# Scheduling edit in a two-layer attention and FFN kernel: fill work, transfers and context turns move to other slots

## The chip, the cores and the metric

The kernel runs on one core of one Trainium2 chip. The time is the device time in microseconds (us) of one execution; lower is better. Engines are named as the profile names them: PE (TensorE), DVE (VectorE), ACT (ScalarE), POOL (GpSimd), SP (SyncE, which issues most DMAs). PEld is PE's weight load.

## The reference, cut to what matters

Two recurrent layers over `x` of shape (2, 512, 512). Layer 0, the one that the change touches, is causal attention with 32 heads of 16 columns and rotary position, times the SiLU of a gated FFN:

```python
xn = _layernorm(x)
q, k, v = split(xn @ qkv_w + qkv_b)           # heads of 16, q and k rotated
probs = softmax(q @ k.T / 4 + causal mask)     # 32 heads, 512 x 512
s = (probs @ v) @ out_w + out_b
g = silu((silu(xn @ W_gate.T) * (xn @ W_up.T)) @ W_down.T)
x = x + s * g
```

Layer 1 (a recurrent convolution stack as "attention" and an octonion ternary FFN) has the same outer form. It takes the time from about 485 us on, and no edit touches it.

## The kernel before, in words

`program` writes one instruction stream by hand for each engine. Layer 0 is done for batch entry b = 0 and then b = 1 (called block 0 and block 1 below).

**Weights as units.** The float32 weights come in 49 units of 128x512 per block. SP loads unit n into `raw[n % 4]` (`load`, L639) once unit n-4 is ready; a high part is made by ACT (`split_hi`, L1263) or by POOL (`split`, L737), and POOL subtracts it for the low part (L745), which makes the unit ready. `HI_BY_ACT` (L178) says up to which unit ACT makes the high part. `w_hi` and `w_lo` have five buffers, so unit n also waits until unit n-5 is used. A product of float32 quality is three matmuls (`passes`, L929: high x high, high x low, low x high); one unit over one of four row chunks is a *triple*, and a unit of Q, K or FFN is four triples.

**Order within a block.** PE does Q unit 0 and K unit 1 of the first eight heads, then the V units 2 to 5, then the first units of `Q_UNIT`, `K_UNIT` and `FFN_UNIT` (L55, L56) "in front" (`fill(b, -1)`, L1027; units 6, 7 and 8, 12 triples, all three FFN). Then come slots s = 0 to 64 (`SLOTS`, L51). Slots 0 to 47 each hold one third of a head pair's scores: PE writes `score_ps` (`scores`, L953) as soon as DVE has taken the row maxima of the slot before from it (`part_ready`, L1037), DVE takes the maxima (`row_maxima`, L1456), and after every third slot joins them (L1467) for PE to turn (`max_turn`, L938). Five slots later PE makes the transposed scores (`scores_T`, L962), ACT takes the exponentials (L1316), POOL masks them (`keep_causal`, L756). After its scores each slot gets *fill*: the triples that `triple_slot` (L80) gives to it, mostly two, in some slots one. When unit u's last triple is in slot s, DVE and ACT do its epilogue in slot s+1: `ffn_tanh` on ACT and `ffn_out` on DVE for the FFN, `rope_first` (three DVE instructions) for Q and K and `rope_second` one slot later. `units_after(s)` lists them. An FFN unit with an even place in `FFN_UNIT` needs ACT's tanh before DVE's `ffn_out`, one with an odd place does not. PE's fill for a unit waits (L988) until the unit two jobs earlier has left its PSUM bank, that is for `ffn_out` or `rope_first` of that one (`proj_free`).

**Stacks.** The rotated Q and K rows go to memory (`write_rows`, L647, in slot `written_in`) and come back as one stack of q and k for each group of four heads (`read_rows`, L657: four DMAs of 200 KB, in slot `read_in`, L113). Group g is needed by PE's scores in slot 6g, which wait for it (L1036). SP does everything in program order, so a load that waits for its unit holds the reads behind it. Group 2 comes from Q and K units 9 and 10; its read is in slot 9, and its scores are in slot 12.

**Context.** `pv_in` gives the product of probabilities and V to slots 12+6g to 15+6g. In slot 16+6g ACT copies it to `ctx_sums` (L1323), in slot 17+6g PE turns that (L1067 to L1070) and DVE divides by the sums (L1590, L1592).

**Down phase.** From slot 54 PE does W_down, one unit f per slot (`down_in`, L117), on `hsh`/`hsl`, which ACT and DVE split from `hidden_T` two slots ahead (L1339, L1607); ACT's split for f needs `down_used` of f-2. PE starts when DVE's first split is there (L1055). The last context groups are turned in slots 53 and 59. ACT makes the high parts of the units that lie behind by `DOWN_HI` (L248).

In these slots PE's order is written out as follows:

```python
fill(b, s)                                       # L1047
max_turn                                         # L1048
down_in(s): wait hs_ready, unit_ready; passes    # L1053
ctx_in(s): wait ctx_copied; turn                 # L1067
pv_in(s)                                         # L1071
```

## Time and profile before

| quantity | value |
|---|---|
| median of 3 runs | 715.39 us |
| lowest, highest | 712.02, 716.94 us |
| profiled execution: its own time | 716.94 us |
| profiled execution: span of its instructions | 715.2 us (1.7 us lie around it) |
| mean granted TensorE clock | 0.97 of full speed |
| PE busy | 637.2 us, 89% of the span |
| DVE, POOL, ACT busy | 433.3, 387.4, 290.9 us |

The profile is of one execution. A timeline row gives the start, the duration, engine, line, operation and the tiles written and read; in brackets stands the idle time of that engine before the row and what ended it. A row of SPq is a DMA issue, and its duration is the issue alone. Matmul ends are modelled, so the distance from one start to the next is the safer figure for them. Stage by stage: the front of block 0 ends at 47.87 us, its slots with scores and fill run to about 197 us, its down phase to 237 us; block 1 has the same at 275, 431 and 470 us.

### The profile page before, as it was taken

What the parts mean: (1) busy time and instruction counts of PE and PEld (TensorE: products, weight loads), DVE (VectorE), ACT (ScalarE), POOL (GpSimd) and SP (SyncE); (2) the same over time, 40 slices, a digit from 0 to 9 for tenths busy, and PEclk for the clock granted to TensorE, in tenths of its full rate; (3) what the DMA queues carried; (4) which work ended last, traced back from release to release, by engine and by line L of the source; (5) the groups of instructions that cost most, each with busy time, mean ns of one, the idle gap of its engine ahead of it and who ended that gap; (6) DMA issues with size and microseconds to landing.
All of it is one profiled execution on the core that took longest, in us unless ns stands there. A gap on an engine that the chain in (4) does not pass through costs nothing. (4 is left out here: it accounts for less than half of the span.)

```text
span 715.2 us, 9831 instructions
## 1 busy us (share of the span) xinstructions
PE 637.2 (89%) x3293; PEld 432.8 (61%) x3293; DVE 433.3 (61%) x1016; ACT 290.9 (41%) x475; POOL 387.4 (54%) x553
## 2 busy tenths in 40 slices
PE   2988899999999998779999999997989799797993
PEld 1855555666567785446566656776765576555671
DVE  4849868666345765966866634567364424657347
ACT  2523545455634430445455553432124334141531
POOL 4665556544333755644645433479426786634465
PEclk9999999999999999989999999999989989999997
DMA  8486755644322335975464337145000000000003
GB/s 287 137 296 189 213 171 162 174 129 103 104 60 66 96 118 164 306 221 167 130 192 134 93 119 301 60 156 184 1 1 0 0 1 1 0 1 0 1 0 117
DMA packets 59906, 83.26 MB, mean 116 GB/s; under 512 B 17848, under 2 KB 26296, under 8 KB 59856
## 3 DMA queue, kind: packets, MB, share of 16 engines
q1 hardware_dynamic: 56192, 71.35, 33.5%
q10 hardware_dynamic: 3664, 11.28, 4.1%
q8 instruction: 26, 0.43, 0.2%
q14 instruction: 24, 0.20, 0.1%
HBM read 64.80 MB, written 26.99 MB: 128 GB/s over the span
## 5 line engine op out<-in xcount | busy, mean ns | idle before, releaser
L745 POOL TENSOR_TENSOR w_lo<-raw,w_hi 128x512 fp32r<-128x512 f32 x98 | 129.7, 1329 | 86.6 <-ACT w_hi L1269 82.2
L1463 DVE CUSTOM_DVE_ANT_0 score_ps<-score_ps,causal 128x512 f32<-128x512 f32 (+3 forms) x256 | 119.8, 515 | 57.0 <-PE score_ps L958 56.5
L1316 ACT ACTIVATE probs_T<-scoreT_ps 128x1024 f32<-128x1024 f32 (+1 forms) x96 | 84.8, 883 | 80.6 <-PE scoreT_ps L967 79.8
L930 PE MATMUL proj_ps<-xn_hi,w_hi 128*128 128x512 f32 x224 | 101.0, 451 | 4.7 <-POOL w_lo L745 2.5
L931 PE MATMUL proj_ps<-xn_hi,w_lo 128*128 128x512 f32 x224 | 89.3, 399 | 0.0
L932 PE MATMUL proj_ps<-xn_lo,w_hi 128*128 128x512 f32 x224 | 89.3, 399 | 0.0
L743 POOL TENSOR_SCALAR w_hi<-raw 128x512 fp32r<-128x512 f32 x50 | 31.0, 620 | 90.4 <-PE proj_ps L932 78.5
L930 PEld LDWEIGHTS proj_ps<-xn_hi,w_hi 128*128 128x128 f32 x224 | 42.4, 189 | 30.2 <-issue 13.1
L958 PE MATMUL score_ps<-k_st,q_st 50*128 50x512 f32 (+3 forms) x256 | 44.7, 386 | 16.9 <-DVE row_max L1463 13.4
L765 POOL TENSOR_SCALAR_AFFINE_SELECT probs_T<-probs_T 128x256 f32<-128x256 f32 x128 | 50.0, 413 | 17.2 <-ACT probs_T L1316 17.1
L958 PEld LDWEIGHTS score_ps<-k_st,q_st 50*128 50x128 f32 x256 | 21.6, 184 | 58.8 <-issue 28.1
L932 PEld LDWEIGHTS proj_ps<-xn_lo,w_hi 128*128 128x128 f32 x224 | 42.9, 192 | 10.1
L1081 PE MATMUL ctx_ps<-probs_T,V 128*32 128x128 f32 (+3 forms) x512 | 47.7, 445 | 0.0
L885 POOL TENSOR_TENSOR hsL<-hidden_T,hsH 128x256 fp32r<-128x256 f32 x44 | 34.8, 803 | 22.2 <-ACT hsH L1402 22.1
L1238 ACT ACTIVATE q_st<-one_turn_ps 2x512 fp32r<-2x512 f32 x64 | 37.4, 584 | 22.0 <-PE one_turn_ps L944 21.7
L931 PEld LDWEIGHTS proj_ps<-xn_hi,w_lo 128*128 128x128 f32 x224 | 42.9, 191 | 5.0
L1516 DVE SCALAR_TENSOR_TENSOR gate_silu<-gate_tanh,proj_ps 128x512 f32<-128x512 f32 x22 | 15.1, 685 | 44.0 <-ACT gate_tanh L1278 38.2
L967 PE MATMUL scoreT_ps<-q_st,k_st 50*128 50x512 f32 (+3 forms) x256 | 37.7, 331 | 1.8 <-ACT probs_T L1316 1.8
L1607 DVE TENSOR_TENSOR hsl<-hidden_T,hsh 128x512 fp32r<-128x512 f32 x22 | 17.0, 771 | 34.6 <-ACT hsh L1339 34.6
L1269 ACT ACTIVATE w_hi<-raw 128x512 fp32r<-128x512 f32 x48 | 29.9, 624 | 17.5 <-PE one_turn_ps L932 6.5
L1247 ACT ACTIVATE rows_hi<-turned_rows 128x512 fp32r<-128x512 f32 x16 | 10.1, 632 | 65.2 <-DVE turned_rows L1544 60.2
L754 POOL TENSOR_TENSOR rows_lo<-turned_rows,rows_hi 128x512 fp32r<-128x512 f32 x16 | 20.8, 1299 | 27.7 <-ACT rows_hi L1247 27.7
(310 smaller groups left out, 1444.8 us busy)
## 6 DMA issues: line engine op xcount, KB each, us to landing
raw<-w SPq DMA_DIRECT2D x98, 256.0 KB, 2.8
rows<-rows_hi SPq DMA_DIRECT2D x32, 256.0 KB, 3.4
arranged<-tern SPq DMA_DIRECT2D x96, 85.0 KB
q_st<-rows SPq DMA_DIRECT2D x32, 200.0 KB
k_st<-rows SPq DMA_DIRECT2D x32, 200.0 KB
rows<-rows_lo SPq DMA_DIRECT2D x16, 256.0 KB, 4.1
gate_w<-arranged ACTq DMA_DIRECT2D x4, 704.0 KB, 7.0
up_w<-arranged ACTq DMA_DIRECT2D x4, 704.0 KB, 7.8
```

The lines of the kernel that those rows point to most:

```text
L745: nc.gpsimd.tensor_tensor(w_lo[n % SPLIT][:, :], raw[n % RAW][:, :], F32(w_hi[n % SPLIT][:, :]), ALU.subtract).then_inc(unit_ready, 1)
L765: m = nc.gpsimd.affine_select(out=halves[:, :, c:c + P], in_=halves[:, :, c:c + P], pattern=[[0, 2], [1, P]], compare_op=ALU.is_ge, fill=0 ...
L885: nc.gpsimd.tensor_tensor(hsL[d % HS][:, :], hidden1_T[:, f, 256 * pr:256 * pr + 256], F32(hsH[d % HS][:, :]), sub).then_inc(hs1_ready, 1)
L930: nc.tensor.matmul(acc, lh, rh, start=first, stop=False)
L931: nc.tensor.matmul(acc, ll, rh, start=False, stop=False)
L932: return nc.tensor.matmul(acc, lh, rl, start=False, stop=last)
L958: m = nc.tensor.matmul(score_ps[:, hh, c:c + (qt + 1) * P], q[:, qt * P:(qt + 1) * P], k[:, 0:(qt + 1) * P], start=part == 0, stop=True, s ...
L967: m = nc.tensor.matmul(scoreT_ps[:, hh, c:c + S - kt * P], k[:, kt * P:(kt + 1) * P], q[:, kt * P:], start=part == 0, stop=True, skip_grou ...
L1081: m = nc.tensor.matmul(ctx_ps[32 * h:32 * h + 32, kt * P:S], V[:, kt, (4 * g + h) * 32:(4 * g + h + 1) * 32], probs_T[(gp + h // 2) % 4][: ...
L1238: m = nc.scalar.activation(q_st[g % 3][64 * hh:64 * hh + 2, j % 2, :], turn_bank(n)[32 * hh:32 * hh + 2, :], ACT.Copy)
L1316: nc.scalar.activation(probs_T[gp % 4][:, c:c + 2 * w].rearrange("p (h c) -> p h c", h=2), scoreT_ps[:, :, 0:w], ACT.Exp, scale=0.25).then ...
L1463: m = nc.vector.tensor_tensor_reduce(out=block, in0=block, in1=causal[:, S - w:], scale=1.0, scalar=-3e38, op0=ALU.add, op1=ALU.max, accum ...
```

## The change

Nine edits, which the diff shows in full:

1. Units 8 and 9 become the second Q and K unit (they were 9 and 10), unit 10 becomes FFN. Eight triples stand in front instead of 12, and the 104 others are spread over the 53 slots. The four that leave the front go to slots 8, 17, 35 and 44, which then hold two triples instead of one. The Q and K units of groups 2 and 3 end in slots 1 and 3 as before; the units behind them up to unit 29 end one slot later, with two exceptions: unit 11 ends in slot 7 (unit 10, FFN now, in slot 5) and unit 12 in slot 9 instead of 7.
2. Group g is read 7 slots after its K unit instead of 6: group 2 in slot 10 instead of 9; the other groups stay in their slots.
3. POOL makes the high parts of units 6, 7 and 8 too.
4. In each slot SP issues the raw loads before the row writes and the stack reads. With edit 1 the load in slot 10 is that of unit 21, which waits for unit 17, and unit 17's split waits for PE's last triple of unit 12 in slot 9. Slot 0 holds seven loads instead of eight.
5. PE turns the context right behind the scores of a slot, ahead of fill and down.
6. PE waits for the last `proj_free` at the first down unit (slot 54) instead of ahead of `norm_turn` (slot 60).
7. ACT copies the context after the tanh, rope, maximum, `hsh` and `DOWN_HI` work of the slot instead of ahead of it.
8. DVE does the `ffn_out` of the front units in slot 0, behind the row maxima of slot 0, instead of ahead of slot 0.
9. ACT no longer makes a high part between the two `rope_hi` of the front.

```diff
--- before.py
+++ after.py
@@ -52,9 +52,8 @@
 
 U_DOWN, U_OUT = 34, 45
 UNITS = U_OUT + KC
-Q_UNIT, K_UNIT, V_UNIT = (0, 9, 12, 18), (1, 10, 13, 19), 2
-FFN_UNIT = [6, 7, 8, 11, 14, 15, 16, 17] + list(range(20, 34))
-IN_FRONT = 3 * KC
+Q_UNIT, K_UNIT, V_UNIT = (0, 8, 12, 18), (1, 9, 13, 19), 2
+FFN_UNIT = [6, 7, 10, 11, 14, 15, 16, 17] + list(range(20, 34))
 FILL = 6
 TRIPLES = (U_DOWN - FILL) * KC
 JOBS = U_DOWN - KC
@@ -79,7 +78,7 @@
 
 def triple_slot(k):
 
-    return max(-1, (k - IN_FRONT) * SCORE_SLOTS // (TRIPLES - IN_FRONT))
+    return max(-1, (k - 2 * KC) * SCORE_SLOTS // (TRIPLES - 2 * KC))
 
 
 def triples_in(s):
@@ -111,7 +110,7 @@
 
 
 def read_in(s):
-    return next((g for g in range(1, GROUPS) if (1 if g == 1 else max(6 * g - 6, unit_slot(K_UNIT[g // 2]) + 6)) == s), None)
+    return next((g for g in range(1, GROUPS) if (1 if g == 1 else max(6 * g - 6, unit_slot(K_UNIT[g // 2]) + 7)) == s), None)
 
 
 def down_in(s):
@@ -175,7 +174,7 @@
 TURN_BANK = turn_banks()
 
 
-HI_BY_ACT = FILL + 3
+HI_BY_ACT = FILL
 RAW_HEAD = 10
 RAW, SPLIT = 4, 5
 COPIES = (50, 49)
@@ -694,12 +693,12 @@
                         write_rows(b, K_UNIT[0])
                         read_rows(b, 0)
                 for s in range(SCORE_SLOTS + 1):
+                    for u in raw_in_slot(s):
+                        load(b, u)
                     for u in written_in(s):
                         write_rows(b, u)
                     if read_in(s) is not None:
                         read_rows(b, read_in(s))
-                    for u in raw_in_slot(s):
-                        load(b, u)
                     if b == 0 and s == 3:
                         write_edges(1)
                     for x in range(copies_in(b, s)):
@@ -1044,6 +1043,10 @@
                         if s > LAG:
                             pe.wait_ge(probs_ready, TASKS * b + s - LAG)
                         scores_T(b, j, x)
+                    if ctx_in(s) is not None:
+                        g = ctx_in(s)
+                        pe.wait_ge(ctx_copied, GROUPS * b + g + 1)
+                        turn(b, ("ctx", g), [ctx_sums[:, t * P:(t + 1) * P] for t in range(NT)])
                     fill(b, s)
                     if max_in(s) is not None:
                         max_turn(b, max_in(s))
@@ -1056,6 +1059,7 @@
                         pe.wait_ge(unit_ready, UNITS * b + U_DOWN + f + 1)
                         if f == 0:
                             pe.wait_ge(probs_ready, TASKS * (b + 1))
+                            pe.wait_ge(proj_free, JOBS * (b + 1))
                         wh, wl = unit(b, U_DOWN + f)
                         for t in range(NT):
                             c = slice(t * P, (t + 1) * P)
@@ -1064,10 +1068,6 @@
                     if s == LAST_DOWN:
                         for kc in range(2, KC):
                             turn(b, ("ctxf", kc), [ctx_rows[:, t, kc * P:(kc + 1) * P] for t in range(NT)])
-                    if ctx_in(s) is not None:
-                        g = ctx_in(s)
-                        pe.wait_ge(ctx_copied, GROUPS * b + g + 1)
-                        turn(b, ("ctx", g), [ctx_sums[:, t * P:(t + 1) * P] for t in range(NT)])
                     if pv_in(s) and pv_in(s)[1] < NT:
                         g, kt = pv_in(s)
                         gp = PAIRS * b + 2 * g
@@ -1084,7 +1084,6 @@
                         if kt == NT - 1:
                             m.then_inc(pv_done, 1)
                     if s == NORM_TURN:
-                        pe.wait_ge(proj_free, JOBS * (b + 1))
                         norm_turn(b + 1)
 
                 for kc in range(KC):
@@ -1284,13 +1283,10 @@
                 split_hi(u)
             magnitudes()
             for b in range(B):
-                for u in range(5 if b else RAW, FILL):
+                for u in range(5 if b else RAW, HI_BY_ACT):
                     split_hi(UNITS * b + u)
                 rope_hi(b, Q_UNIT[0])
-                split_hi(UNITS * b + FILL)
                 rope_hi(b, K_UNIT[0])
-                for u in range(FILL + 1, HI_BY_ACT):
-                    split_hi(UNITS * b + u)
                 act.wait_ge(ones_set, 2 + b)
                 for i in range(NT):
                     act.wait_ge(v_done, NT * b + i + 1)
@@ -1315,12 +1311,6 @@
                         w, c = WIDTH[x], t_col(0, x)
                         nc.scalar.activation(probs_T[gp % 4][:, c:c + 2 * w].rearrange("p (h c) -> p h c", h=2), scoreT_ps[:, :, 0:w], ACT.Exp,
                                              scale=0.25).then_inc(probs_ready, 1)
-                    if pv_in(s) and pv_in(s)[1] == NT:
-                        g = pv_in(s)[0]
-                        act.wait_ge(pv_done, GROUPS * b + g + 1)
-                        if g:
-                            act.wait_ge(turned, use(b, ("ctx", g - 1)) + 1)
-                        nc.scalar.activation(ctx_sums[:, :], ctx_ps[:, :], ACT.Copy).then_inc(ctx_copied, 1)
                     for u in units_after(s):
                         if u in FFN_OF:
                             ffn_tanh(b, u)
@@ -1340,6 +1330,12 @@
                     for u in range(U_DOWN, UNITS):
                         if s == DOWN_HI[u - U_DOWN]:
                             split_hi(UNITS * b + u)
+                    if pv_in(s) and pv_in(s)[1] == NT:
+                        g = pv_in(s)[0]
+                        act.wait_ge(pv_done, GROUPS * b + g + 1)
+                        if g:
+                            act.wait_ge(turned, use(b, ("ctx", g - 1)) + 1)
+                        nc.scalar.activation(ctx_sums[:, :], ctx_ps[:, :], ACT.Copy).then_inc(ctx_copied, 1)
                     if s == TASKS:
 
                         act.wait_ge(rows_lo_ready, 8 * (b + 1))
@@ -1571,8 +1567,6 @@
                         dve.wait_ge(tern_a, w + 1)
                         nc.vector.scalar_tensor_tensor(out=tern_neg[w][:, :], in0=tern_w[w][:, :], scalar=theta[:, 1, w:w + 1], in1=tern_over[w][:, :],
                                                        op0=ALU.is_lt, op1=ALU.subtract).then_inc(tern_ready, 1)
-                for u in units_after(0):
-                    ffn_out(b, u)
                 for s in range(SLOTS):
                     if score_in(s):
                         row_maxima(b, s)
@@ -1596,7 +1590,7 @@
                     for u in units_after(s - 1):
                         if u in QK_OF:
                             rope_second(b, u)
-                    for u in units_after(s) if s else ():
+                    for u in units_after(s):
                         if u in FFN_OF:
                             ffn_out(b, u)
                         else:
```

## Rows read from the trace of the kernel before

**Rows 1.** Busy time by stretch: us, engines (instructions), granted clock, DMA share, GB/s.

```profile
47.87:84.87 37.00, 30.62 (x157) 19.38 (x156) 33.42 (x94) 12.92 (x18) 21.70 (x28) 1.00 0.65 200
...
275.00:318.60 43.60, 32.99 (x155) 20.80 (x155) 33.53 (x94) 14.08 (x21) 28.67 (x35) 0.92 0.72 232
...
44.20:47.60 3.40, 3.40 (x10) 2.52 (x8) 0.00 (x0) 0.00 (x0) 3.32 (x4) 0.50 1.04 411
...
310.30:317.00 6.70, 5.21 (x17) 3.34 (x16) 3.14 (x7) 1.97 (x3) 2.54 (x5) 0.51 0.93 285
```

**Rows 2.** Timeline of PE, block 0, end of the front and slots 0, 1.

```profile
43.37 0.47 PE L930 MATMUL proj_ps<-xn_hi,w_hi 128*128 128x512 f32 x1 [2.12 <-DVE gate_silu L1516]
...
47.87 0.49 PE L958 MATMUL score_ps<-k_st,q_st 50*128 50x512 f32 x2
...
50.72 0.50 PE L958 MATMUL score_ps<-k_st,q_st 50*128 50x384 f32 x4 [0.76 <-DVE row_max L1463]
```

**Rows 3.** Timeline of SP's queue: stack reads of groups 0 and 2, both blocks.

```profile
34.28 0.71 SPq L668 DMA_DIRECT2D q_st<-rows  x2
...
72.49 0.92 SPq L668 DMA_DIRECT2D q_st<-rows  x2
...
267.81 0.70 SPq L668 DMA_DIRECT2D q_st<-rows  x2
...
306.46 0.70 SPq L668 DMA_DIRECT2D q_st<-rows  x2
```

**Rows 4.** Timeline of PE, block 1: slot 0, its fill, slot 12.

```profile
274.99 0.50 PE L958 MATMUL score_ps<-k_st,q_st 50*128 50x512 f32 x2 [0.37 <-DMA k_st<-rows]
...
277.63 0.50 PE L930 MATMUL proj_ps<-xn_hi,w_hi 128*128 128x512 f32 x1 [2.14 <-POOL w_lo L745]
...
313.03 0.79 PE L958 MATMUL score_ps<-k_st,q_st 50*128 50x512 f32 x2 [1.49 <-DMA k_st<-rows]
```

**Rows 5.** Timeline of DVE, block 0: first row maxima of slot 0.

```profile
49.27 0.69 DVE L1463 CUSTOM_DVE_ANT_0 score_ps<-score_ps,causal 128x512 f32<-128x512 f32 x1
```

**Rows 6.** Timeline of ACT, block 0: exponentials of slot 6.

```profile
66.86 1.00 ACT L1316 ACTIVATE probs_T<-scoreT_ps 128x1024 f32<-128x1024 f32 x1
```

**Rows 7.** Timeline of DVE, block 0: epilogue of slot 6.

```profile
67.47 0.68 DVE L1520 TENSOR_TENSOR hidden_T<-gate_silu,proj_ps 128x512 f32<-128x512 f32 x1
```

**Rows 8.** Timeline of POOL, block 0: high part of unit 17.

```profile
70.09 0.62 POOL L743 TENSOR_SCALAR w_hi<-raw 128x512 fp32r<-128x512 f32 x1 [0.70 <-PE proj_ps L932]
```

**Rows 9.** Timeline of PE, block 0: scores of slots 10, 12, 23, 25.

```profile
76.13 0.50 PE L958 MATMUL score_ps<-k_st,q_st 50*128 50x384 f32 x4 [1.97 <-DVE row_max L1463]
...
81.15 0.50 PE L958 MATMUL score_ps<-k_st,q_st 50*128 50x512 f32 x2
...
112.98 0.39 PE L958 MATMUL score_ps<-k_st,q_st 50*128 50x256 f32 x2 [0.48 <-DVE row_max L1463]
...
120.52 0.50 PE L958 MATMUL score_ps<-k_st,q_st 50*128 50x384 f32 x4 [1.20 <-DVE row_max L1463]
```

**Rows 10.** Timeline of ACT, block 0: slot 52, then slot 58.

```profile
196.16 0.59 ACT L1323 ACTIVATE ctx_sums<-ctx_ps 128x512 f32<-128x512 f32 x1
...
215.75 0.63 ACT L1339 ACTIVATE hsh<-hidden_T 128x512 fp32r<-128x512 f32 x1 [1.67 <-PE score_ps L932]
...
216.29 0.62 ACT L1269 ACTIVATE w_hi<-raw 128x512 fp32r<-128x512 f32 x1
```

**Rows 11.** Timeline of PE, block 0: slots 53, 54, then slot 59.

```profile
196.81 0.66 PE L926 MATMUL one_turn_ps<-ident,ctx_sums 128*128 128x128 f32 x4 [0.28 <-ACT ctx_sums L1323]
...
198.12 0.50 PE L930 MATMUL score_ps<-w_hi,hsh 128*128 128x512 f32 x1 [0.66 <-DVE hsl L1607]
...
215.49 0.39 PE L930 MATMUL score_ps<-w_hi,hsh 128*128 128x512 f32 x1
...
218.22 0.60 PE L926 MATMUL one_turn_ps<-ident,ctx_sums 128*128 128x128 f32 x4
```

**Rows 12.** Timeline of DVE, block 0: slot 53.

```profile
198.61 0.68 DVE L1520 TENSOR_TENSOR hidden_T<-gate_silu,proj_ps 128x512 f32<-128x512 f32 x1
```

## The prediction, made before the changed kernel was seen

> **What bounds the kernel now.** I read the busy time by stretch first. In the slots of block 0 from 47.87 to 84.87 us PE is busy for 30.6 of 37.0 us and DVE for 33.4; in the same slots of block 1 (275.00 to 318.60) PE is busy for 33.0 of 43.6 us, at a granted clock of 0.92 [rows 1]. So the first dozen slots are not bound by PE: its idle time there ends on DVE's row maxima, on the stack read of group 2 (1.49 us at 313.03) or, in the front, on DVE and POOL [rows 2, 4, 9]. Every other stretch of layer 0 is PE's, and there each us that PE newly waits lengthens the kernel. The timelines then say which step holds PE at each place that the change touches. I work with the profiled execution (716.94 us, 1.55 above the median of 715.39) and carry the difference over to the median.
>
> **Fewer triples in front.** In block 0 PE waits 2.12 us before the third front unit, and its scores begin at 47.87 [rows 2]. After the change they can follow unit 7, which ends before the wait, at 43.37 - 2.12 = 41.25, if the stack is there. The stack of group 0 in block 1 is first issued at 267.81, and the scores that wait for it start at 274.99: 7.2 us [rows 3, 4]. From 34.28 that gives 41.5. But slot 0's fill is now unit 8, whose bank rule wants the `ffn_out` of unit 6, and DVE does that behind slot 0's row maxima. Scores 0.5; maxima 1.45 (from 49.27 to the release of slot 1 at 50.72 [rows 2, 5]); `ffn_out` 0.7 [rows 7]: PE resumes at 44.15. A triple takes 0.7: four triples of the down phase span 215.49 to 218.22 [rows 11]. Two of them put slot 1 at 45.55 instead of 50.72: **5.2 earlier**. That new wait has PE's whole queue behind it.
>
> In block 1 the stack is the limit already: 274.99 stays. The fill resumes at 274.99 + 0.5 + 1.45 + 0.7 = 277.6, where it resumed before (277.63, then for unit 9's low part [rows 4]). **Nothing is gained**, though four triples less are done.
>
> POOL's extra high parts (three of 0.62 [rows 8] per block) end before PE wants these units in block 0 and lie under the wait for the stack in block 1; ACT's freed time was idle too. Cost 0; if not covered, 3 x 0.62 = 1.9 per block.
>
> **Slots 1 to 10.** From slot 1 to slot 10 block 0 takes 76.13 - 50.72 = 25.4. Slot 10 loses its wait for row maxima of 1.97, since the rope of unit 12 moves from slot 8 to slot 10 [rows 9]. Slot 8 holds one triple more, +0.7. Slot 6 loses an epilogue that needs no tanh (DVE at 67.47) and gets one that does: ACT can make the tanh only behind its exponentials, which end at 67.86 [rows 6, 7], and with 0.6 of tanh DVE starts at about 68.4, +0.9. So 25.4 - 2.0 + 0.7 + 0.9 = 25.0: slot 10 starts at 70.6.
>
> **The read of group 2.** This is the term that speaks against the change. Before, POOL starts unit 17's high part at 70.09, as soon as PE is through with unit 12, SP loads raw unit 21 when unit 17 is ready, and the read goes out at 72.49: 2.4 us [rows 3, 8]. Now unit 12 ends two slots later, the load is in slot 10, and the read stands behind it. Unit 12 ends shortly before slot 10, so the split starts at about 70.4 and the read goes out at 72.8. The nearest flight is block 1's: issued at 306.46, scores released at 313.03, 6.6 us [rows 3, 4]; the other one is 7.2. The stack lands at 79.4, while slot 12 would be due at 70.6 + (81.15 - 76.13) = 75.6 [rows 9]. PE stands for 3.8 us, and slot 12 starts 1.75 before the 81.15 of now. Of the 5.2 gained, this is what is left.
>
> Block 1, with the same steps from 279.1 (277.6 and two triples): slot 10 at 304.1, read at 306.3, slot 12 at 312.9 against 313.03 [rows 4]. **About 0**, though its old stall was only 1.49. The row writes of unit 9 go out earlier than before there, since fewer loads stand ahead of them in slot 0; I take that as enough for the read not to wait for them.
>
> **The deferred triples.** Of the four, slot 8's is counted. The three of slots 17, 35 and 44 lie where PE doesn't wait: 3 x 0.7 = **+2.1 per block**.
>
> **The later ropes.** Units 18 and 19 move a slot on. The waits for row maxima at 112.98 (0.48) and 120.52 (1.20) [rows 9] become, with the ropes beside longer slots, about 0.6 in all: **-1.1 per block**. Bounds: 0 and -1.7. The earlier context turn frees DVE sooner in these slots, and PE doesn't wait for it, as ACT copies without tanh or rope ahead of it in them.
>
> **The down phase.** Two new waits, both on PE, and PE is the bound.
> - Slot 54 waits for the last `proj_free`. DVE's instruction for it runs from 198.61 to 199.29 (it stands behind the context work), while PE started at 198.12 [rows 11, 12]. PE starts at 199.4: **+1.3**. The turn of slot 53 gets later by one `hsh` (0.6), within this wait.
> - Slot 59: ACT's `hsh` of slot 58 can start only when PE ends slot 58 (215.75, after a wait for PE), then comes a high part to 216.91, and only then, now, the context copy of 0.59 [rows 10]: 217.5. PE wants the turn, now ahead of its down unit, at 215.49 [rows 11]. **+2.0.** Before, the copy was ahead of `hsh`, and the turn at 218.22 waited for nothing. Queued behind PE's wait are all down units left and the next block's norm turns, so nothing gives it back. Bounds for both together: 0, were the waits covered in some way, and 5.
>
> So +3.3 per block. The wait taken out of slot 60 ended nowhere: 0.
>
> **The clock.** In two stretches the granted clock is 0.50, that is the 1.2 GHz level: 44.20 to 47.60, right behind PE's wait of 2.12 (3.4 us, price 1.7), and 310.30 to 317.00 around the stall of group 2 in block 1 (6.7 less 1.49 idle, halved: 2.6) [rows 1, 2, 4]. Behind the 2.14 at 277.63 no such stretch followed. After the change the wait of block 0's front is as long, block 1's slot 12 stalls longer, and block 0's slot 12 stalls anew. I take one half-speed stretch more than now, **+1.7**; bounds 0 and five more (8.5).
> The Trainium skill ("TensorE: Matmul & The Clock Gate", section "HAM oscillation — how this bites in real kernels") says that a PE that waits for a DMA between bursts drops to the low clock, and that the next burst then starts cold each time. By it both stalls at slot 12 and the wait for the first stack of block 1 would be paid at the low clock. The rows agree for 313.03 and say nothing of a 3.8 us stall; this rule is the second rival below.
>
> **The sum.** Block 0: -1.75 + 2.1 - 1.1 + 3.3 = +2.55. Block 1: 0 + 2.1 - 1.1 + 3.3 = +4.3. Clock +1.7. Total **+8.5**: 725.4 on the profiled execution, 723.9 on the median, 1.2% slower.
>
> **The rivals.**
> 1. *The group 2 read isn't late.* If it flew in less time or were waited for by less, slot 12 would start when due: 3.8 earlier in block 0, and in block 1 at 304.1 + 5.0 = 309.1, 3.8 earlier. 8.5 - 7.6 = +0.9, 716.3: not slower. For it: the two flights differ by 0.6, so the DMA share of the moment counts, and fewer loads are queued here. Against: two flights of 6.6 and 7.2 with two slots of about 5 us to cover them. It decides from a flight below 2.8 us.
> 2. *Cold bursts.* Three more half-speed stretches than the one counted, 3 x 1.7 = +5.1: 729.0. For it: 3.8 us stalls are longer than any wait of now in these slots. Against: 277.63.
> 3. *The down phase hides its waits.* 8.5 - 6.6 = +1.9: 717.3. For it: DVE and ACT are half idle there. Against: the order of the two queues is written out, and each wait names an instruction with a row.
> 4. *Both 1 and 3*: the early start pays and nothing takes it back, 8.5 - 7.6 - 6.6 = -5.7: 709.7, faster.
>
> **How the numbers follow.** Chances: forecast 0.45, rival 1 0.17, rival 2 0.16, rival 3 0.12, rival 4 0.10. About 1% (7.2 us) is what a measurement of this kernel can tell from no change. The forecast, with some 3 us either way, is beyond 722.5 in two cases of three (0.30) and within it else (0.15); rival 2 adds 0.16 to slower, rivals 1 and 3 give 0.26 to no change and 0.03 to slower, and rival 4 is split between faster (0.06) and no change (0.04). That makes 0.49 slower, 0.45 same, 0.06 faster. The range runs from 714.5 (rival 1 with the clock's term gone) to 730.
>
> **What would show it.** PE's scores of slot 12 wait 3 to 4.5 us for the DMA `k_st` in both blocks, and SP issues the read of group 2 about 2.4 us behind POOL's start on unit 17. Slot 0's scores are at about 41.5 and 275. PE's first down matmul waits for DVE's `hidden_T`, about 2.3 us in all with the turn, and the turn of slot 59 waits 2 us for ACT's `ctx_sums`. If the down waits are absent the step on program order is wrong; if slot 12 doesn't wait, the one on the flight; if both stand and the time is beyond 730, the clock's.

## The result: 3% slower, beyond the range

| quantity | before | after |
|---|---|---|
| median | 716.16 us (4 runs, 712.02 to 720.77) | 737.43 us (4 runs, 734.84 to 739.20) |
| ratio after / before, 95% interval | | 1.029 [1.022, 1.037] |
| profiled execution, its span | 716.94, 715.2 us | 734.26, 732.5 us |
| PE busy | 637.2 us | 644.0 us |
| PE not busy (span less busy) | 78.0 us | 88.5 us |
| mean granted clock | 0.970 | 0.953 |

The forecast was 723.9 us within 714.5 to 730: the sign is right, the size is not. The medians lie 21.3 us apart and the two profiled executions 17.3; the account below is of the profiled pair, and it doesn't cover the other 4 us (the executions of one kernel lie 2 to 12 us apart). The last rows of the table split the 17.3 us by which the span grew. PE stands 10.5 us longer, and it is busy for 6.8 us longer although not one matmul was added (3293 in both). The second part is what to explain: the same matmuls took longer.

Two rows of the page of after, the totals and the slices of PE's clock:

```profile
PE 644.0 (88%) x3293; PEld 437.5 (60%) x3293; DVE 434.5 (59%) x1016; ACT 288.4 (39%) x469; POOL 392.1 (54%) x559
...
PEclk9999899999999998989999998999999989898997
```

The waits of PE in after (for what, us in total, times, longest):

```profile
PE score_ps L957 <- DMA k_st<-rows: 13.6, 3, 5.3
...
PE score_ps L957 <- DVE row_max L1459: 8.3, 10, 2.0
...
PE one_turn_ps L925 <- ACT ctx_sums L1338: 5.2, 4, 1.8
...
PE score_ps L929 <- DVE hidden_T L1516: 3.0, 2, 1.5
```

The same view of the kernel before:

```profile
PE score_ps L958 <- DVE row_max L1463: 13.4, 14, 2.0
...
PE score_ps L958 <- DMA k_st<-rows: 3.1, 3, 1.5
...
PE score_ps L930 <- DVE hsl L1607: 1.3, 2, 0.7
...
PE one_turn_ps L926 <- ACT ctx_sums L1323: 0.6, 2, 0.3
```

Waits for row maxima shrank by 5.1 us; waits for the stack grew by 10.5, and those of the down phase from 1.9 to 8.2. All three places were named in the prediction. PE's timeline of after has them one by one (start, duration, what PE did, and in brackets the idle time ahead of it); these rows answer to [rows 2, 4, 9, 11]:

```profile
40.21 0.50 PE L957 MATMUL score_ps<-k_st,q_st 50*128 50x512 f32 x2
42.84 0.77 PE L929 MATMUL proj_ps<-xn_hi,w_hi 128*128 128x512 f32 x1 [2.13 <-POOL w_lo L744]
43.40 0.63 PE L930 MATMUL proj_ps<-xn_hi,w_lo 128*128 128x512 f32 x1
43.83 0.63 PE L931 MATMUL proj_ps<-xn_lo,w_hi 128*128 128x512 f32 x1
...
45.67 0.50 PE L957 MATMUL score_ps<-k_st,q_st 50*128 50x384 f32 x2
...
79.72 0.80 PE L957 MATMUL score_ps<-k_st,q_st 50*128 50x512 f32 x2 [5.31 <-DMA k_st<-rows]
...
198.77 0.66 PE L925 MATMUL one_turn_ps<-ident,ctx_sums 128*128 128x128 f32 x4 [0.79 <-ACT ctx_sums L1338]
200.93 0.47 PE L929 MATMUL score_ps<-w_hi,hsh 128*128 128x512 f32 x1 [1.50 <-DVE hidden_T L1516]
201.23 0.39 PE L930 MATMUL score_ps<-w_hi,hsl 128*128 128x512 f32 x1
201.46 0.39 PE L931 MATMUL score_ps<-w_lo,hsh 128*128 128x512 f32 x1
...
220.20 0.65 PE L925 MATMUL one_turn_ps<-ident,ctx_sums 128*128 128x128 f32 x4 [1.78 <-ACT ctx_sums L1338]
...
280.59 0.49 PE L957 MATMUL score_ps<-k_st,q_st 50*128 50x512 f32 x2 [3.25 <-DMA k_st<-rows]
283.21 0.76 PE L929 MATMUL proj_ps<-xn_hi,w_hi 128*128 128x512 f32 x1 [2.13 <-DVE gate_silu L1512]
...
321.10 0.80 PE L957 MATMUL score_ps<-k_st,q_st 50*128 50x512 f32 x2 [5.08 <-DMA k_st<-rows]
```

Two things are to be seen. Every place holds the wait that the step on it foresaw, and the two at slot 12 are longer than reckoned. And the distance between two matmuls of one chain is not the same everywhere: 0.23 us at 201.23, 0.43 at 43.40. The second is a matmul at the low clock. The busy time by stretch shows how much of that there is; these are all half-speed stretches of layer 0 in after:

```profile
42.41:45.82 3.41, 2.98 (x8) 1.99 (x8) 0.97 (x2) 0.00 (x0) 3.24 (x5) 0.50 1.04 405
56.06:59.48 3.42, 3.42 (x11) 2.06 (x10) 3.33 (x11) 1.55 (x2) 0.81 (x1) 0.50 0.92 308
76.54:83.37 6.83, 3.65 (x12) 2.80 (x13) 3.39 (x8) 1.65 (x2) 2.39 (x4) 0.50 0.94 264
281.34:288.17 6.83, 4.96 (x13) 3.48 (x14) 3.70 (x13) 0.00 (x0) 6.50 (x8) 0.50 0.39 123
318.89:325.71 6.82, 4.61 (x16) 3.26 (x16) 3.51 (x7) 1.57 (x2) 2.38 (x4) 0.50 0.91 253
441.77:448.59 6.82, 5.83 (x16) 4.00 (x20) 1.71 (x3) 0.28 (x1) 1.17 (x1) 0.50 1.01 409
sum 34.13, PE 25.45 PEld 17.59 DVE 16.63 ACT 5.05 POOL 16.49; mean PE 4.24 PEld 2.93 DVE 2.77 ACT 0.84 POOL 2.75
```

Before had two of them, with PE busy for 3.40 + 5.21 = 8.6 us in them [rows 1]; after has six, with 25.45 us. A matmul at 1.2 GHz comes every 0.43 us and not every 0.23 to 0.24, so some 45% of this busy time is lost: 11.4 us instead of 3.9, **+7.5 us** (with a plain half, +8.4). The prediction had allowed +1.7.

The 45% hold where PE is the bound. PE's busy time in layer 0 grew by less, 5.2 us (452.1 to 457.4), so +7.5 is an upper value and +5.2 a lower one; after_again below shows where a part of the difference goes.

The account stage by stage, both profiles:

| stretch | before | after | difference |
|---|---|---|---|
| start to first scores of block 1 | 274.99 | 280.59 | +5.6 |
| block 1 to the turn of layer 1's first input | 222.6 (274.99 to 497.58) | 232.7 (280.59 to 513.28) | +10.1 |
| layer 1 | 217.6 | 219.2 | +1.6 |

The 1.6 us of layer 1 are the clock again. The sums over the half-speed stretches behind 497.58 us of before, then behind 513.28 us of after:

```profile
sum 23.89, PE 21.02 PEld 15.71 DVE 11.47 ACT 4.82 POOL 13.71; mean PE 4.21 PEld 3.14 DVE 2.29 ACT 0.96 POOL 2.74
sum 27.31, PE 24.81 PEld 19.18 DVE 12.66 ACT 7.32 POOL 14.10; mean PE 4.96 PEld 3.84 DVE 2.53 ACT 1.46 POOL 2.82
```

PE works 3.8 us more at half speed there, and 45% of that is 1.7. No kernel of this document changes layer 1, and yet it lasts 215.9 to 221.5 us in their 14 profiles. PE's work at half speed in it is 17.2 to 29.5 us, each us of it goes with 0.46 us of layer 1's length, and no profile lies more than 0.1 us off that line.

### The profile page after: what moved, and what is told of

Same layout as the page of the kernel before. It is cut to its first block and busy times, and to the rows that moved or that the text cites. A ratio compares the mean times of both kernels' runs of the same rounds, so it can differ in the third digit from the quotient of the medians.

```text
span 732.5 us, 9833 instructions
## 1 busy us (share of the span) xinstructions
PE 644.0 (88%) x3293; PEld 437.5 (60%) x3293; DVE 434.5 (59%) x1016; ACT 288.4 (39%) x469; POOL 392.1 (54%) x559
## 5 line engine op out<-in xcount | busy, mean ns | idle before, releaser
L744 POOL TENSOR_TENSOR w_lo<-raw,w_hi 128x512 fp32r<-128x512 f32 x98 | 127.8, 1307 | 95.0 <-ACT w_hi L1268 90.1
L742 POOL TENSOR_SCALAR w_hi<-raw 128x512 fp32r<-128x512 f32 x56 | 37.1, 663 | 99.3 <-PE proj_ps L931 90.5
L1237 ACT ACTIVATE q_st<-one_turn_ps 2x512 fp32r<-2x512 f32 x64 | 37.5, 585 | 26.9 <-PE one_turn_ps L943 26.4
L1246 ACT ACTIVATE rows_hi<-turned_rows 128x512 fp32r<-128x512 f32 x16 | 10.1, 631 | 75.1 <-DVE turned_rows L1540 75.1
L1459 DVE DVE_READ_ACCUMULATOR2_ANT row_max<- 128x1 f32 x256 | 35.6, 139 | 0.3
L1329 ACT ACTIVATE hsh<-hidden_T 128x512 fp32r<-128x512 f32 x22 | 13.9, 630 | 49.9 <-PE score_ps L931 49.9
L1268 ACT ACTIVATE w_hi<-raw 128x512 fp32r<-128x512 f32 x42 | 26.2, 624 | 17.0 <-PE one_turn_ps L931 6.3
```

The lines of the kernel that those rows point to most:

```text
L742: nc.gpsimd.tensor_scalar(w_hi[n % SPLIT][:, :], raw[n % RAW][:, :], 1.0, 0.0, ALU.mult, ALU.add).then_inc(hi_done, 1)
L744: nc.gpsimd.tensor_tensor(w_lo[n % SPLIT][:, :], raw[n % RAW][:, :], F32(w_hi[n % SPLIT][:, :]), ALU.subtract).then_inc(unit_ready, 1)
L1237: m = nc.scalar.activation(q_st[g % 3][64 * hh:64 * hh + 2, j % 2, :], turn_bank(n)[32 * hh:32 * hh + 2, :], ACT.Copy)
L1459: m = nc.vector.tensor_tensor_reduce(out=block, in0=block, in1=causal[:, S - w:], scale=1.0, scalar=-3e38, op0=ALU.add, op1=ALU.max, accum ...
```

## The experiments

Twelve runs, one of them of the changed kernel once more. "Before" was run again beside each group on the same chip (medians 714.63, 717.67 and 716.38 us), and every ratio is against it. Two theories stand against each other. By the prediction's, the held read and the two down waits cost their own lengths. By the other, here called the clock theory, the new waits are paid a second time, through matmuls at the low clock. A third question is which edit owns which wait.

### undo4: the order of SP's queue put back

```diff
-                    for u in raw_in_slot(s):
-                        load(b, u)
                     for u in written_in(s):
                         write_rows(b, u)
                     if read_in(s) is not None:
                         read_rows(b, read_in(s))
+                    for u in raw_in_slot(s):
+                        load(b, u)
```

> The changed kernel with SP's order put back (row writes and stack reads ahead of the raw loads of a slot). Theory A (the read of group 2 is late because raw unit 21 stands ahead of it, and the long PE waits also bring half-speed stretches): SP gets to the read as soon as the copies of slot 9 are out, about 69 to 70 us in block 0 instead of 72.5; it lands at about 76, PE's wait at slot 12 falls from 5.3 to some 1.5 us in both blocks, and with it at least one of the two half-speed stretches there. 7.6 us of waits and 2 to 4 us of clock: about 727 where the changed kernel has 737. Rival B (the read isn't held by the load but by the row writes' landing or by DMA traffic, so the order of issue doesn't matter): the wait at slot 12 stays near 5 us and the time at 737.

Measured: 729.39 us, 1.019 [1.013, 1.024]. Its interval just touches that of after (1.029 [1.022, 1.037]). The stalls at slot 12 shrank from 5.31 and 5.08 to 3.32 and 2.17 us, not to the 1.5 that was expected. SP's and PE's timelines of undo4 show why they did not go:

```profile
69.03 1.94 SPq L707 DMA_DIRECT2D arranged<-tern  x2
71.02 0.92 SPq L667 DMA_DIRECT2D q_st<-rows  x2
```

```profile
79.85 0.80 PE L957 MATMUL score_ps<-k_st,q_st 50*128 50x512 f32 x2 [3.32 <-DMA k_st<-rows]
```

The same two views of after:

```profile
72.12 0.33 SPq L644 DMA_DIRECT2D raw<-w  x1
72.50 0.77 SPq L667 DMA_DIRECT2D q_st<-rows  x2
```

In after the read goes out behind raw unit 21, 0.4 us later, as the prediction had it. With the old order it is no longer behind this load, but still behind slot 9's load and slot 9's two copies of ternary weights (edit 2 put it in slot 10; undo24567 below takes that back too). Counted from slot 0 (at 41.61 here, 40.21 in after) it goes out 2.9 us earlier, but then 8.8 us pass until the scores are released instead of 7.2, so slot 12 comes only 1.3 us earlier behind slot 0. In block 1 the read goes out 2.3 us earlier and slot 12 comes 2.9 earlier. So edit 4 is a cause. Why the flight of block 0 was longer is open.

### undo57: both context edits put back

```diff
-                    if ctx_in(s) is not None:
-                        g = ctx_in(s)
...
                     fill(b, s)
...
+                    if ctx_in(s) is not None:
+                        g = ctx_in(s)
...
                     if pv_in(s) and pv_in(s)[1] < NT:
...
+                    if pv_in(s) and pv_in(s)[1] == NT:
+                        g = pv_in(s)[0]
...
                     for u in units_after(s):
...
-                    if pv_in(s) and pv_in(s)[1] == NT:
-                        g = pv_in(s)[0]
...
```

PE turns the context behind the down unit again, and ACT copies it ahead of tanh, rope and `hsh`.

> The changed kernel with the context copy of ACT and the context turn of PE put back in their old places; the proj_free wait stays at the first down unit. Theory A: the 1.78 us wait for ctx_sums at slot 59 goes in both blocks and that at slot 53 falls from 0.8 to 0.3; the wait for hidden_T at slot 54 stays or grows to 2 us, since it hangs on DVE. 2 x 1.8 to 2 x 2.3 us, plus the half-speed stretch of 6.8 us at 441.8 if it was the slot 59 wait that brought it (2.9): 731 to 734. Rival C (the turn of the context ahead of the fill pays in slots 17 to 47 by freeing DVE): going back costs more there than the down phase gives, 737 or above.

Measured: 732.38 us, 1.024 [1.020, 1.029]. PE's waits of undo57:

```profile
PE score_ps L929 <- DVE hidden_T L1516: 3.9, 2, 2.0
```

PE's waits for `ctx_sums` are back at 0.6 us in all, so the one of slot 59 is gone (1.78 us in each block). The first down matmul waits for DVE in full, 1.97 us instead of 0.79 + 1.50: the context turn had only been in front of that wait. So edits 5 and 7 own the slot 59 term, edit 6 the slot 54 one (1.97 + 0.29 us, against 0.66 + 0.28 in before). This rests on the waits: by its time undo57 isn't told apart from the changed kernel, whose second run below has 1.025 [1.018, 1.031].

### undo4567: the four edits of order put back, the new unit order kept

Beside the edits of undo4 and undo57 the `proj_free` wait goes back:

```diff
                         if f == 0:
                             pe.wait_ge(probs_ready, TASKS * (b + 1))
-                            pe.wait_ge(proj_free, JOBS * (b + 1))
...
                     if s == NORM_TURN:
+                        pe.wait_ge(proj_free, JOBS * (b + 1))
                         norm_turn(b + 1)
```

> The changed kernel with SP's order, both context edits and the proj_free wait put back: what is left is fewer triples in front, the later read rule, the high parts on POOL, and the late ffn_out of the front. Theory A: of the 21 us, 7.6 (waits at slot 12), 6.2 (down phase) and most of the added half-speed time go: 717 to 721. Rival D (the four triples that left the front are what costs, with all that they shift, and the waits are its symptoms): it stays above 725.

Measured: 720.80 us, 1.009 [1.005, 1.012] (10 runs): of the 3% about 1% is left, and rival D falls. The down phase is that of before (0.65 us at the first down matmul); slot 12 still waits 2.17 and 1.68 us for its stack.

### only567: before with the context edits and the `proj_free` edit alone

The diff is the reverse of those of undo57 and undo4567, applied to the kernel before; units and SP's order stay.

> The kernel before with only the two context edits and the proj_free wait. Theory A: +1.3 us at slot 54 and +1.8 to +2.0 at slot 59 in each block, 6.4 in all, and up to two half-speed stretches of 6.8 us behind them (2.5 to 2.9 each): 722 to 728, ratio 1.009 to 1.017. Rival C (the early turn frees DVE in the slots 17 to 47 and pays): ratio 1.00 or below, with the down waits there all the same.

Measured: 727.20 us, 1.016 [1.009, 1.022], that is +12.6 us on the median of before (714.63). Rival C falls: the kernel is slower. The waits of the down phase are those of after within 0.02 us, in PE's timeline of only567:

```profile
114.71 0.66 PE L926 MATMUL one_turn_ps<-ident,ctx_sums 128*128 128x128 f32 x4 [1.43 <-ACT ctx_sums L1342]
...
197.96 0.66 PE L926 MATMUL one_turn_ps<-ident,ctx_sums 128*128 128x128 f32 x4 [0.81 <-ACT ctx_sums L1342]
...
200.11 0.47 PE L930 MATMUL score_ps<-w_hi,hsh 128*128 128x512 f32 x1 [1.50 <-DVE hidden_T L1520]
```

With 1.78 at slot 59, less the 0.28 and 0.66 that before waits at slots 53 and 54 [rows 11], this is +3.1 us per block, 6.3 in all. The first row is a wait that neither before nor after has: in slot 23 the early turn waits 1.43 us for ACT's copy (1.42 in block 1), and the 1.20 for row maxima two slots on [rows 9] are gone in return. In the profiles PE stands 83.8 us against 78.0 of before, 5.9 more, so the other half of the growth is not waiting: PE is busy 6.0 us longer. Three of the six half-speed stretches of layer 0 in only567, by busy time, and the sum of the six:

```profile
43.71:47.12 3.41, 3.41 (x10) 2.64 (x9) 0.04 (x1) 0.00 (x0) 3.24 (x4) 0.50 1.04 407
115.39:118.80 3.41, 3.41 (x12) 2.16 (x11) 3.31 (x7) 0.18 (x1) 1.21 (x3) 0.50 0.81 230
...
282.64:289.47 6.83, 5.22 (x14) 3.67 (x15) 1.93 (x10) 0.00 (x0) 6.50 (x8) 0.50 0.36 93
...
sum 23.89, PE 22.28 PEld 15.65 DVE 8.72 ACT 0.44 POOL 11.92; mean PE 3.71 PEld 2.61 DVE 1.45 ACT 0.07 POOL 1.99
```

22.28 us of PE work at half speed against 8.6 of before: 45% of the difference is 6.1 us. Layer 0 is 10.6 us longer than in before's profile (508.20 - 497.58) and layer 1 1.3 us, so 6.3 + 6.1 is again a little too much for layer 0. The 12.6 of the medians has an interval of 6.6 to 15.5 us and tests no more than the size. The clock theory has both halves, the prediction's only one.

### after_again and warm: the same waits with the clock kept up

after_again is the changed kernel without an edit, to stand beside warm on one chip.

> The changed kernel unchanged, beside the next three on the same chip: 735 to 739.

Measured: 735.26 us, 1.025 [1.018, 1.031]. Its profile is a second one of the same kernel, and has five half-speed stretches in layer 0, the first at 78.84 us. Its busy time up to there and the sum of the five, then slot 12 in PE's timeline:

```profile
18.40:78.80 60.40, 48.65 (x230) 35.29 (x228) 46.26 (x109) 23.05 (x38) 41.87 (x44) 1.00 0.67 211
...
sum 30.73, PE 27.31 PEld 17.68 DVE 12.29 ACT 4.29 POOL 10.64; mean PE 5.46 PEld 3.54 DVE 2.46 ACT 0.86 POOL 2.13
```

```profile
78.98 0.79 PE L957 MATMUL score_ps<-k_st,q_st 50*128 50x512 f32 x2 [5.21 <-DMA k_st<-rows]
```

Here the stretches of after at 42.41 and 56.06 are missing, which 45% prices at 2.9 us. Slot 0 is 1.3 us shorter without them (40.09 to 44.25, against 40.21 to 45.67), but slot 12 comes 38.9 us behind slot 0 against 39.5 in after, only 0.6 less: PE waits 4.3 us for row maxima on the way instead of 2.1. In slots that DVE bounds, most of the price was not paid.

warm puts matmuls that nothing reads into PE's waits (into banks that are free there): 14 ahead of block 1's first stack, 9 ahead of slot 0's fill, 24 ahead of slot 12, 7 ahead of the first down unit, 8 ahead of slot 59's turn. The diff shows the first and third of these places:

```diff
+                        if s == 12 or (b and s == 0):
+                            if s:
+                                pe.wait_ge(part_ready, TASKS * b + s)
+                            for _ in range(24 if s else 14):
+                                nc.tensor.matmul(score_ps[:, 0, :], xn_hi[:, 0, 0:P], xn_hi[:, 0, :], start=True, stop=True)
                         if s % 6 == 0:
```

> The changed kernel with matmuls added whose result nobody reads, in PE's waits: 9 ahead of slot 0's fill, 14 ahead of block 1's wait for its first stack, 24 ahead of slot 12's wait, 7 ahead of the first down unit, 8 ahead of slot 59's turn. The waits themselves stay, so the work of the kernel ends no sooner by order. Theory A (long waits of PE bring the half-speed stretches, and these are the part of the slowdown that the prediction missed): the stretches at 42, 76, 281, 319 and 442 us go or shrink, some 34 us at half speed in layer 0 become under 12, and the time falls by 6 to 10 us, to 727 to 731, against after_again. Rival E (the half-speed stretches come by themselves, whatever PE does, or their cost lies under other waits): the same time as after_again or 1 to 3 us more, for the added matmuls.

Measured: 726.66 us, 1.013 [1.008, 1.019]; beside after_again, 8.6 us less, with 110 matmuls more. Four runs each, with their spread, leave some 5 us either way on that. Slot 12 of block 0 starts no earlier than in after (79.72), in PE's timeline of warm:

```profile
74.91 5.74 PE L1037 MATMUL score_ps<-xn_hi 128*128 128x512 f32 x24 [0.80 <-DVE row_max L1474]
80.58 0.50 PE L957 MATMUL score_ps<-k_st,q_st 50*128 50x512 f32 x2
```

The busy time of warm over the whole of layer 0, one row:

```profile
18.40:509.80 491.40, 468.24 (x2632) 318.93 (x2630) 316.11 (x855) 212.29 (x325) 264.75 (x378) 1.00 0.52 154
```

The granted clock is 1.00 from 18.40 to 509.80 us: not one half-speed stretch, where after has six and after_again five. Nothing else was changed, and SP issues the read at 72.21, as in after (72.50). In the profiles layer 0 is 8.4 us shorter than in after_again (layer 1 begins at 507.07 instead of 515.43). By 45% the 27.3 us at half speed had cost 12.3 there; the 110 matmuls take 26 us (0.24 each), while PE's idle time in layer 0 fell by 21.9 (57.6 to 35.7), so some 4 us of the gain go back to them, at slot 12 above all, where the filler and not the stack ends last. This decides for the clock theory. The 8.6 us are what all half-speed stretches of layer 0 cost less the fillers, and not the added ones alone.

### undo8: `ffn_out` of the front units ahead of slot 0 again

```diff
+                for u in units_after(0):
+                    ffn_out(b, u)
                 for s in range(SLOTS):
...
-                    for u in units_after(s):
+                    for u in units_after(s) if s else ():
```

> The changed kernel with DVE's ffn_out of the two front units ahead of slot 0 again. Theory A: PE's fill of slot 0 follows its scores at once in block 1 and 0.6 us earlier in block 0, but slot 12 is held by the read of group 2, which hangs on unit 12, so about 2 us come back in block 1 up to slot 10 and pass on to the read: -2 to -3 us in all, and one half-speed stretch (281) less, -2.4: 732 to 735. Rival F (the late ffn_out is the main cost, by all that shifts behind it): 728 or below.

Measured: 732.58 us, 1.021 [1.015, 1.027], beside after_again's 1.025 [1.018, 1.031]: not told apart. Rival F falls. Slot 0 of block 1 takes 3.0 us instead of 5.5. Slot 12 still waits 4.98 us there (5.50 in block 0), but the gain isn't lost in that wait: the read hangs on PE's own unit 12, goes out 3 us earlier behind slot 0, and slot 12 comes 37.5 us behind slot 0 instead of 40.5 in after and 40.6 in after_again. Block 0 gives nothing, 40.5 against 39.5 and 38.9. So edit 8 may own up to 3 us of the loss, which the spread of four runs hides.

### only1: before with the new unit order alone, a miss

```diff
-Q_UNIT, K_UNIT, V_UNIT = (0, 9, 12, 18), (1, 10, 13, 19), 2
-FFN_UNIT = [6, 7, 8, 11, 14, 15, 16, 17] + list(range(20, 34))
-IN_FRONT = 3 * KC
+Q_UNIT, K_UNIT, V_UNIT = (0, 8, 12, 18), (1, 9, 13, 19), 2
+FFN_UNIT = [6, 7, 10, 11, 14, 15, 16, 17] + list(range(20, 34))
```

> The kernel before with only the new order of units (eight triples in front instead of 12, Q and K of groups 2 and 3 one unit earlier), everything else as it was: read rule, SP's order, ffn_out ahead of slot 0, high parts on ACT. Theory A: scores begin at about 41 in block 0; the read of group 2 in slot 9 stands behind raw unit 20 only and lands in time, so slot 12 waits under 1 us in both blocks; down phase as before. Block 0 gains 5.6 us at slot 12 and gives 2.0 back for the triples, block 1 gains about 4 in slots 0 to 12 and gives 2.0 back: 706 to 712, faster than both. Rival D (fewer triples in front cost in themselves): 716 or above.

Measured: 718.83 us, 1.001 [0.997, 1.004] (12 runs). No gain, though block 0 did what was expected of it: slot 12 starts at 75.22 instead of 81.15, waiting for row maxima only. Part of these 5.9 us is the clock: only4 and before_x below do the same as before up to there, have no half-speed stretch in it, and start slot 12 at 78.18 and 78.65. Block 1 lost the gain. PE's timeline of only1, slot 12 of block 0, then slots 0 and 12 of block 1, then SP's timeline in block 1 and a row of SP's waits:

```profile
75.22 0.50 PE L957 MATMUL score_ps<-k_st,q_st 50*128 50x512 f32 x2 [0.89 <-DVE row_max L1462]
...
272.69 0.49 PE L957 MATMUL score_ps<-k_st,q_st 50*128 50x512 f32 x2 [3.44 <-DMA k_st<-rows]
...
309.04 0.79 PE L957 MATMUL score_ps<-k_st,q_st 50*128 50x512 f32 x2 [5.31 <-DMA k_st<-rows]
```

```profile
292.40 1.76 SPq L714 DMA_DIRECT2D X<-x  x4
294.20 1.17 SPq L652 DMA_DIRECT2D rows<-rows_hi  x2
...
301.70 0.71 SPq L667 DMA_DIRECT2D q_st<-rows  x2
```

```profile
SPq L667 <- DMA rows<-rows_lo: 9.4, 3, 4.6
```

Block 1 has transfers that block 0 has not: `X` is loaded in slot 6, right ahead of the row writes of unit 9. The read is now early enough to wait for those writes (4.6 us), and PE waits behind it, as long as in after. Two half-speed stretches lie there, one behind a wait of 2.02 for row maxima (284.75 to 288.16) and one at slot 12 (308.64 to 315.47), and layer 1 lasts 221.5 us instead of 217.6, with 29.5 us of PE's work at half speed instead of 21.0.

### undo24567: the read rule put back as well

```diff
-    return next((g for g in range(1, GROUPS) if (1 if g == 1 else max(6 * g - 6, unit_slot(K_UNIT[g // 2]) + 7)) == s), None)
+    return next((g for g in range(1, GROUPS) if (1 if g == 1 else max(6 * g - 6, unit_slot(K_UNIT[g // 2]) + 6)) == s), None)
```

> As undo4567 (SP's order, context edits and proj_free wait put back), and the read rule put back too: group 2 is read in slot 9 again, ahead of slot 9's two copies. Theory A (what stands ahead of the read on SP sets when it lands): block 0 issues it some 2.5 us earlier than undo4567 and the wait at slot 12 (2.17 us there) falls under 0.3; block 1 keeps about 1.5 us or more, since there the row landing of unit 9 behind the X loads holds the read. 1 to 3 us below undo4567's 720.8: 717 to 720. Rival G (the flight is bound by DMA traffic): the wait stays at 2 us and the time at 721.

Measured: 718.67 us, 1.004 [1.000, 1.007] (10 runs). The read goes out at 66.46 instead of 71.17 in undo4567, so edit 2 is a cause too, and slot 12 waits 0.9 us for row maxima, in neither block for a DMA. What stays in place of the 3% is 0.4%: edits 2, 4, 5, 6 and 7 carry the loss, edit 8 at most together with them.

### only4: before with SP's new order alone

```diff
                 for s in range(SCORE_SLOTS + 1):
+                    for u in raw_in_slot(s):
+                        load(b, u)
                     for u in written_in(s):
```

> The kernel before with only SP's order changed. The read of group 2 is in slot 9, where no load stands, so the load ahead of it changes nothing; those of groups 3 to 5 get a load ahead in slots 12, 18 and 24, which are due six slots later. Theory A: no difference (ratio 0.996 to 1.004), no wait at slot 12 of block 0. Rival H (the order of loads and row writes costs by itself): slower by 3 us or more.

Measured: 718.63 us, 1.002 [0.999, 1.006] (8 runs). By itself the order that costs 2 to 3 us of stall per block in the changed kernel costs nothing measurable: with before's units no load in the read's slot waits for a late unit. Its harm is its meeting with edits 1 and 2.

### before_x and only1_x: the traffic of `X` moved out of the way

In both, block 1 stores `X` in slot 13 instead of 2 and loads it in slot 20 instead of 6; before_x is the kernel before with this, only1_x is only1 with it.

```diff
-                    if b == 1 and s == 2:
+                    if b == 1 and s == 13:
                         sp.wait_ge(combined, 2 * NT)
...
-                    if b == 1 and s == 6:
+                    if b == 1 and s == 20:
                         sp.wait_ge(x2_stored, 16)
```

> The kernel before, with block 1's store of the old X moved from slot 2 to 13 and the loads of the new X from slot 6 to 20. Theory A: unit 9's and 10's row writes no longer stand behind 2 MB of X traffic, the read of group 2 lands before slot 12 is due, ACT's rope isn't held at slot 9: waits of 1.42 and 1.49 us and the half-speed stretch at 310 (2.5) go: 3 to 5 us faster, ratio 0.992 to 0.997. Rival G: no change.

> only1 (the new order of units alone on the kernel before) with the same move of the X store and loads. Theory A: block 1's wait of 5.3 us at slot 12 falls to under 2 us and the half-speed stretch of 6.8 us at 308.6 goes: 5 to 7 us faster than only1, 711 to 714, ratio to before 0.990 to 0.995. Rival D (fewer triples in front cost in themselves): no faster than before_x and before, since the wait moves elsewhere.

Measured: before_x 715.97 us, 1.002 [0.999, 1.005] (12 runs), a miss: the DMA wait at slot 12 of block 1 is gone, but two half-speed stretches lie in that execution at 274.21 (6.83 us) and 304.93 (3.41 us), and the time is the same. only1_x 713.84 us, 0.997 [0.995, 0.998] (12 runs, before 716.38): slot 12 of block 1 in PE's timeline of only1_x:

```profile
309.91 0.51 PE L957 MATMUL score_ps<-k_st,q_st 50*128 50x512 f32 x2 [0.90 <-DVE row_max L1462]
```

The 5.31 us for the stack in only1 are gone: it was the `X` traffic that held unit 9's row writes. This version is faster than both kernels, by 0.3% against before, less than the 0.5 to 1% that was expected. The early start of block 0 was worth 3.0 to 3.4 us at slot 12 (75.22 in only1, against 78.18 and 78.65 at the same clock), and the three deferred triples behind it take 1.9 of them back; 2.5 us arrive from both blocks.

## Why the prediction was wrong in size and right in place

Step by step. The first three rows are times of the profile as they stand; in the differences behind them the clock is told apart, at 45% of PE's busy time at half speed:

| term | predicted | measured in the profile of after |
|---|---|---|
| slot 1, block 0 | 45.55 | 45.67 |
| read of group 2 issued | 72.8 | 72.50 |
| slot 12, block 0 | 79.4, waiting 3.8 | 79.72, waiting 5.31 |
| slot 12, block 1, against slot 0 | 0 | +2.5, of which 1.7 clock |
| three deferred triples | +2.1 per block | +1.9: slots 17, 35, 44 are 0.65, 0.52, 0.69 longer |
| later ropes | -1.1 per block | about -0.2 |
| down phase | +3.3 per block | +3.1 (0.79 + 1.50 + 1.78 less 0.94) |
| clock, layer 0 | +1.7 | +7.5 at 45%: 3.0 in block 0, 4.5 in block 1; +5.2 by PE's busy time |
| layer 1 | 0 | +1.6, the clock too |

The steps on program order held. **The held read**: rivals 1 and 4 fell, from the issue to the released scores it took 7.2 us (72.50 to 79.72). PE came 1.2 us sooner to slot 12 than reckoned (79.72 - 5.31 = 74.4, not 75.6), and waited longer for the same end. **The down phase**: rival 3 fell, each wait is within 0.3 us of its step, and undo57 and only567 show which edit owns which.

**The step that failed is the clock**: "I take one half-speed stretch more than now, +1.7". The runs showed four more in layer 0, with 16.8 us more of PE's work in them (25.45 against 8.6), which is +5.2 to +7.5, and 3.8 us more in layer 1, +1.6, where the prediction had put nothing and given no reason. Rival 2 had the mechanism, but its price was wrong as well (three more stretches, 729.0), for three reasons that the rows show. A stretch here lasts 3.4 or 6.8 us, and four of after's six are of the longer kind; the prediction priced each at 3.4. It let the rule speak for DMA waits alone, while the stretches at 42.41, 56.06 and 441.77 stand by waits of 2.13 for POOL, 1.96 for DVE's row maxima and 0.80 + 1.50 for ACT and DVE. And it took the wait of 2.14 at 277.63, which no half-speed stretch followed, as evidence against, though the other one, of 2.12, was followed by one [rows 2, 4]. One of two is no evidence of absence, and the change has seven waits of 1.5 us or more that before lacks or has shorter. Its upper bound, five more, 8.5 us, would have held the value of layer 0. The test was written down beforehand (both waits stand and the time is beyond 730: the clock's step is wrong); that is what came, and warm shows it: 8.6 us given back by filling the waits, with no wait ended earlier.

With the Trainium skill ("TensorE: Matmul & The Clock Gate", section "HAM oscillation — how this bites in real kernels"), which says that each burst behind a DMA wait starts cold, the trace of after agrees: the stretches at 76.54 and 318.89 begin in a wait for the stack, the one at 281.34 right behind such a wait, in the next one. "Each" goes too far: in only1 PE waits 3.44 us for the first stack of block 1, until 272.69, and the granted clock stays at 1.00 until 284.75. And the rule is about waits for DMAs, while here stretches also stand by waits of some 2 us for POOL and DVE.

**The smaller miss** is the later ropes, 0.9 us per block: with them a slot on, PE waits 0.52 and 0.62 us for row maxima and 0.30 for ACT in slots 24 to 27, instead of the 0.48 and 1.20 of [rows 9]. The wait moved to the neighbours and did not shrink.

Summed again with these values, block 0 gives 2.55 + 0.9 + 3.0 = 6.5 (measured 5.6), block 1 4.3 + 0.9 + 4.5 = 9.7 (10.1), layer 1 has 1.6: 17.8 against 17.3 us of span. That block 0 comes out 0.9 too high fits after_again, where slots bound by DVE did not pay the whole price.

What stays open: why one wait is followed by a half-speed stretch and the next of the same length is not. This moves whole executions: by layer 1 alone, which no edit touches, the profiles differ by 5.7 us. So the 4 us by which the medians differ more than the profiled pair can't be placed, and the 0.4% of undo24567 rests on ten runs and is near its bound.

## What to carry to other kernels

Price every new wait of a PE-bound stretch twice: once for its length and once for the matmuls behind it at the low clock; in this kernel 10.5 us more of waiting came with 6.8 us more of busy time for the same matmuls, and waits of 2 us for a neighbour engine could be followed by slow matmuls like waits for a DMA. The second price is due only where PE is the bound. On a queue that goes in program order, look at what stands ahead of a latency-bound read and what that in turn waits for: an order that is harmless alone (only4) delayed the read by 2 to 3 us once the units behind it were renumbered, and a gain in one place (only1) was lost to a transfer that only the other block has. If a wait can't be removed, matmuls that nothing reads can keep the clock up: 110 of them took 8.6 us off here (some 5 us either way).

## What the runs showed of the hardware that was not expected

- A matmul at the 1.2 GHz level costs 0.43 us against 0.23 to 0.24, a factor of 1.8 and not 2; half of the busy time overstates the loss a little. Layer 1's length in 14 profiles gives the same price, 0.46 us for each us that PE works at half speed.
- The clock was often still low, or fell, when PE was busy again: 441.77 to 448.59 begins in the second of two waits of 0.80 and 1.50 and has PE busy for 5.83 of 6.82 us, and in only567 the stretch at 115.39, 0.7 us behind the end of a wait of 1.43, has PE busy throughout.
- Whether a given wait is followed by such a stretch changes with when it comes: before_x has one at 304.93, right behind a wait of 1.90 for row maxima; before has the same wait (1.89, until 304.94), no stretch behind it, and one at 310.30 instead. A single profile is a sample of this, and predictions are better made with the expected number of stretches than with the places of one trace.
